# Block lists for a top-1 expert layer: one-hot products in PSUM in place of a table in DRAM

## What is computed

```
x = x + linear_attention(layernorm(x))                 # 0: K^T V form, head of 64
x = x + routed_ffn(layernorm(x)) + shared_ffn(...)     # 0: 8 experts, top 2, inner 352; shared inner 704
x = x + windowed_attention(layernorm(x))               # 1: 16 heads of 16, |i-j| <= 128
logits = xf @ Wg + bg                                  # 1: the last layer
one_hot = one_hot(argmax(logits))
h = gelu(einsum('td,edh->eth', xf, W1)); y = einsum('eth,ehd->etd', h, W2)
out = x + einsum('etd,te->td', y, one_hot)             # 8 experts, top 1, inner 1024
```

## Time and profile before

| | us |
|---|---|
| median of three runs | 1680.56 |
| lowest and highest | 1666.24, 1683.63 |
| the profiled execution | 1689.96 |
| its span on the core | 1688.1 |

### The profile page before, as it was taken

One profiled execution on the slowest core, in us unless ns is written; L12 is line 12 of the kernel. 1 busy time (PEld: TensorE's weight loads), 2 busy tenths in 40 slices (PEclk: granted clock), 3 DMA queues, 4 the chain that ended last, 5 costly groups with the idle time before them and its releaser, 6 DMA issues.

```text
span 1688.1 us, 23687 instructions
## 1 busy us (share of the span) xinstructions
PE 1485.8 (88%) x7821; PEld 1074.7 (64%) x7821; DVE 694.9 (41%) x2367; ACT 458.3 (27%) x769; POOL 481.8 (29%) x568
## 2 busy tenths in 40 slices
PE   7999999999999998988887888888968897688896
PEld 4666655677777764555655555555646786588886
DVE  5643355233333333567775666656543011000000
ACT  1111110112211111145544443535334411111111
POOL 2100000342222215134343343524233432333331
PEclk9998999999999999989998988879878998799999
DMA  9201000111222112335434344434233866678784
GB/s 336 83 17 50 9 0 1 40 61 61 62 63 63 59 53 76 92 106 147 119 114 92 111 98 131 105 110 115 73 79 121 243 174 211 224 291 296 291 312 171
DMA packets 90326, 205.05 MB, mean 121 GB/s; under 512 B 12712, under 2 KB 46783, under 8 KB 80224
## 3 DMA queue, kind: packets, MB, share of 16 engines
q1 hardware_dynamic: 72656, 168.19, 32.0%
q0 software_dynamic: 13184, 32.17, 6.4%
q10 hardware_dynamic: 4368, 3.17, 0.6%
HBM read 151.50 MB, written 52.38 MB: 121 GB/s over the span
## 4 chain that ended last, share of the span: by engine, by line
PE 75%; DMA 8%; DVE 6%; issue 5%; ACT 3%; POOL 1%; SPq 1%; ACTq 1%; DVEq 0%; POOLq 0%
PE psum L699 10%; PE psum L581 9%; PE psum L870 9%; PE psum L880 8%; PE psum L678 5%; PE psum L592 5%; DMA qT<-max_T 4%; PE psum L770 4%; PE psum L725 4%; PE psum L747 3%; PE psum L797 3%; PE psum L508 2%; PE psum L826 1%; PE psum L660 1%; DVE work L1655 1%
## 5 line engine op out<-in xcount | busy, mean ns | idle before, releaser
L1655 DVE CUSTOM_DVE_ANT_0 work<-psum,mask 128x384 bf16<-128x384 f32 (+1 forms) x512 | 230.1, 487 | 183.3 <-PE psum L725 174.6
L1105 ACT ACTIVATE arena<-psum 128x512 f32<-128x512 f32 (+1 forms) x256 | 179.2, 703 | 249.1 <-PE psum L747 237.6
L725 PE MATMUL psum<-kz,qT 96*128 96x384 f32 (+1 forms) x512 | 184.7, 442 | 15.3 <-DVE small L1655 12.3
L699 PE MATMUL psum<-arena,work 128*128 x568 | 186.6, 472 | 3.0 <-ACT work L1017 2.4
L870 PE MATMUL psum<-arena 128*128 128x128 f32 x1248 | 154.9, 285 | 26.5 <-issue 17.1
L747 PE MATMUL psum<-qT,kz 100*128 100x384 f32 (+1 forms) x512 | 136.6, 349 | 39.6 <-DMA qT<-max_T 27.3
L870 PEld LDWEIGHTS psum<-arena 128*128 128x128 f32 x1248 | 150.0, 200 | 31.5 <-issue 22.0
L1731 POOL DMA_INDIRECT work<-normed,token_of x71 | 67.3, 948 | 352.1 <-PE psum L660 210.6
L725 PEld LDWEIGHTS psum<-kz,qT 96*128 96x128 f32 x512 | 97.6, 214 | 98.8 <-issue 50.8
L581 PE MATMUL psum<-arena 128*128 128x512 f32 x320 | 154.3, 628 | 0.0
L1528 DVE TENSOR_TENSOR arena<-psum,arena 128x256 f32<-128x256 f32 x39 | 16.6, 425 | 315.1 <-PE psum L880 315.1
(11 more groups left out here) (216 smaller groups left out, 2021.5 us busy)
## 6 DMA issues: line engine op xcount, KB each, us to landing
arena<-in_w SPq DMA_DIRECT2D x78, 1024.0 KB, 7.8
strips<-hi SPq DMA_DIRECT2D x64, 256.0 KB
kz<-strips SPq DMA_DIRECT2D x64, 192.0 KB, 4.0
qT<-strips SPq DMA_DIRECT2D x32, 384.0 KB, 5.7
results<-work SPq DMA_DIRECT2D x71, 128.0 KB, 1.7
strips<-lo SPq DMA_DIRECT2D x32, 256.0 KB
normed<-work SPq DMA_DIRECT2D x14, 512.0 KB, 3.4
X<-in_x SPq DMA_DIRECT2D x8, 512.0 KB, 9.7
```

The lines of the kernel that those rows point to most:

```text
L699: m = e.matmul(psum[:, pair[u], 0:INTER], xsT0[:, b % 2, c * P:(c + 1) * P], wu0[:, bass.ds(x, 1), c, u * INTER:(u + 1) * INTER], start=(c ...
L725: m = e.matmul(psum[:, bk, at:at + w], qT[0:ROWS_S, slot, half, i * P:(i + 1) * P], kz[slot][0:ROWS_S, hd, lo_key:hi_key], start=True, sto ...
L1105: e.activation(pT[:, j, 2 * half:2 * half + 2, 0:w], src, ACT.Exp, scale=1.0 / E ** 0.5).then_inc(p_exped, 1)
L1655: e.tensor_tensor_reduce(masked[:, n % 2, 0:w], psum[:, bank_of["scores", u, i, hd], at:at + w], mask[:, P - off:P - off + w], 1.0, MASKED ...
```

## The change

The table in DRAM goes, with its clearing, the 32 indirect writes of `pool_place`, the two gathers of `pool_list` and the turning of `pe_list`. In place of them:

- `dve_slots` splits each slot into a place in its block and a block row (`places`), three more small operations a batch.
- `dve_list` loses the six operations that found the table's row and gains four that find each listed block's row number (`block_row`).
- `dve_list_piece` makes, for four token tiles at a time, a one-hot matrix of the places (`one_r`, 128 x 4 x 128) and one of the blocks, twice more multiplied with the tile's number and the row's number (`one_b`, 128 x 4 x 3 blocks). `pe_list_piece` multiplies them into one PSUM bank, four bf16 matmuls a piece. The first list has 5 pieces, one a step (114 to 118), the second 8, two a step (162 to 165); PE does each one step later. `dve_tokens` (steps 120 and 167) takes five dependent small operations in place of two.
- The bank of the first list is bank 2, one of three that the scores use, so the units whose steps overlap it (28 and 29) have two banks.
- SP issues the first weights of block k+1 ahead of the second weights of block k.
- The early blocks are laid later: their first products at 129, 132, 135, 138, 141, 145, 150, 154, 159, 161, 163, 165 (before: 129, 131, 133, 135, 137, 139, 141, 144, 149, 153, 159, 162) and their second at 133, 136, 139, 143, 147, 152, 156, 160, 162, 164, 166, 168 (before: 132 to 145, then 150, 154, 160, 163, 166). The late blocks start at step 170, before at 168.

```diff
-LATE_AT = LISTED_AT[1] + 7
+ROWS_AT = [128, 129, 132, 135, 138, 141, 145, 150, 154, 159, 161, 163]
+UP_AT = ROWS_AT[1:] + [165]
+DOWN_AT = [133, 136, 139, 143, 147, 152, 156, 160, 162, 164, 166, 168]
+LATE_AT = LISTED_AT[1] + 9
+PIECES_AT = [[LISTED_AT[0] + 1 + n for n in range(EARLY_B * TPB // CH)],
+             [LISTED_AT[1] + 1 + n // 2 for n in range(NT // CH)]]
+FETCH_AT += [max(at - 4, PIECES_AT[1][-1] + 2) for at in ROWS_AT[EARLY:]]
...
         def s_ring(u):
-            return (0, 1, 2) if u else (0, 1)
+            return (0, 1) if u in (0, *LIST_UNITS) else (0, 1, 2)
...
+        def pe_list_piece(e, i, n):
+            w, last = 3 * (EARLY, NBLK1 - EARLY)[i], len(PIECES_AT[i]) - 1
+            if n == 0:
+                fill(e, ("list", i), LIST_BANK[i])
+            m = i * len(PIECES_AT[0]) + n
+            e.wait_ge(ones_made, m + 1)
+            for t in range(CH):
+                p = e.matmul(psum[:, LIST_BANK[i], 0:w], one_r[m % 2][:, t, :],
+                             one_b[m % 2].rearrange("p t k b -> p t (k b)")[:, t, 0:w],
+                             start=(n == 0 and t == 0), stop=(n == last and t == CH - 1))
...
+        def dve_list_piece(e, i, n):
...
+            e.tensor_tensor(one_r[m % 2], repeat(count[:, :]), spread(places[:, 0, ts], P), ALU.is_equal)
+            e.tensor_tensor(one, repeat(block_row[:, 0:w]), spread(places[:, 1, ts], w), ALU.is_equal).then_inc(one_hot_made, 1)
+            e.wait_ge(one_hot_made, m + 1)
+            e.tensor_tensor(tile_no, one, spread(count[:, ts], w), ALU.mult)
+            e.tensor_scalar(row, one, row_no[:, 0:1], None, ALU.mult).then_inc(ones_made, 1)
...
-            e.tensor_scalar(slot_of[:, 2, b * TPB:(b + 1) * TPB], slot1, float(NX * NT * P), None, ALU.add).then_inc(slotted, 1)
+            dve_then(e, e.tensor_scalar(slot_int, slot1, float(NX * NT * P), None, ALU.add))
+            e.tensor_scalar(place_i[:, 0, :], slot_int, P - 1, None, ALU.bitwise_and)
+            dve_then(e, e.tensor_scalar(place_i[:, 1, :], slot_int, P.bit_length() - 1, None, ALU.arith_shift_right))
+            e.tensor_copy(places[:, :, b * TPB:(b + 1) * TPB], place_i).then_inc(placed, 1)
...
-                for b, _ in batch(s, GATE_AT + 4):
-                    pool_place(e, b)
-                for i in range(2):
-                    if s == LISTED_AT[i] + 2:
-                        pool_list(e, i)
...
+            sp_first_weights(e, 0)
             for k in range(NBLK1):
-                sp_weights(e, k)
+                if k + 1 < NBLK1:
+                    sp_first_weights(e, k + 1)
+                sp_second_weights(e, k)
```

More of the change, by code:

```diff
@@ L133, in blocks_at, with piece @@
     return [k for k in range(NBLK1) if at[k] + behind == step]
+def piece(step, behind=0):
+    return [(i, n) for i in range(2) for n, at in enumerate(PIECES_AT[i]) if at + behind == step]
 def later(step, behind=0):
@@ L264, in build @@
         y1 = carve(arena, 29952, 3, E)
[L267 to L279, removed]
+        PAD = 2 * NT * P
+        sc1, eq1, cand1, hot1 = (carve(arena, 15168 + TPB * NX * i, TPB, NX) for i in range(4))
+        places = carve(arena, 15296, 2, NT)
+        (so_far, in_batch, n_tokens, n_blocks, up_to, offset, taken, least, jump) = (
+            carve(arena, 15360 + NX * i, NX) for i in range(9))
+        best, pick, rank, slot1 = (carve(arena, 15432 + TPB * i, TPB) for i in range(4))
+        place_i = carve(arena, 15448, 2, TPB).bitcast(I32)
+        block_row = carve(arena, 15456, NBLK1)
+        found = [carve(arena, 15456 + NBLK1 * (1 + i), NBLK1) for i in range(2)]
+        n_int, slot_int = n_tokens.bitcast(I32), slot1.bitcast(I32)
+        NB1 = max(EARLY, NBLK1 - EARLY)
+        ends = carve(work, 4512, NB1, NX)
+        which = carve(work, 4512 + NB1 * NX, NB1)
+        one_r = [carve(work, 4768 + i * CH * P // 2, CH * P // 2).bitcast(BF16)
+                 .rearrange("p (t r) -> p t r", t=CH) for i in range(2)]
+        one_b = [carve(work, 5280 + i * CH * 3 * NB1 // 2, CH * 3 * NB1 // 2).bitcast(BF16)
+                 .rearrange("p (t k b) -> p t k b", t=CH, k=3) for i in range(2)]
         xn = carve(work, 0, 2, TPB, E)
@@ L1513, in dve_tokens @@
         def dve_tokens(e, i):
             n, first = (EARLY, NBLK1 - EARLY)[i], (0, EARLY)[i]
-            bk = bank_of["list", i]
+            tile_no, row, one = (psum[:, LIST_BANK[i], k * n:(k + 1) * n] for k in range(3))
+            f = [found[k][:, 0:n] for k in range(2)]
             e.wait_ge(*done["list", i])
-            e.tensor_copy(token_out[:, first:first + n], psum[:, bk, 0:n])
-            e.tensor_scalar(token_of[:, 1, first:first + n], psum[:, bk, 0:n], NT * P - 1.0, None, ALU.min
-                            ).then_inc(tokens_listed, 1)
+            e.tensor_copy(f[0], row).then_inc(tokens_found, 1)
@@ L1522, in dve_result @@
+            e.wait_ge(tokens_found, 4 * i + 4)
+            e.tensor_copy(token_out[:, first:first + n], f[0]).then_inc(tokens_listed, 1)
         def dve_result(e, k):
@@ L1587, in dve_attention @@
                         dve_list(e, i)
+                for i, n in piece(s):
+                    dve_list_piece(e, i, n)
                 for u, i in unit(s, 0, 4):
```

108 lines of the change are left out of this document (48 added, 60 removed).

## The result

| | before | after |
|---|---|---|
| median, us (four runs each) | 1675.39 | 1589.49 |
| lowest to highest | 1666.24 to 1683.63 | 1582.57 to 1593.92 |
| profiled execution, us | 1689.96 | 1582.57 |

The ratio is 0.9485, 95% interval 0.9416 to 0.9553: 86 us faster, where 54 were forecast, to 1627 us, and 1604 was the lower end of the range. The direction was right and the size was not.

The account below looks back on a forecast made before the run. PE, busy for 88% of the span, was taken as the bound, with its idle time and slow clock to be won. The terms 8 + 9 - 1 + 5 + 14 + 19 = 54 us took 1680.56 to 1627 us, range 1604 to 1658.

Parts of the forecast that it names:

- The writes into the table: In the attention's batches: without 4-byte table writes DMAs land sooner and PE waits less; 9 us won, from 2 to 14.
- Late blocks: Late blocks: first weights issued 3.5 us sooner remove most of PE's 23.1 us of waits before first products; 19 us won.
- First list: At the first list: 15.4 us on offer less 7.5 for pieces, banks and PE's matmuls; net 8, between 3 and 14.
- Early blocks: Stretch from 1290 us: PE's idle of 17 us becomes about 12; change -5 us, between -9 and +5.
- Second list: End of the ranks to first late product: overhead falls from 22 to 8 us; 14 won, between 10 and 17.
- The DMA ceiling (2): Rival, chance 0.2: late blocks limited by bytes, 7.7 to 8.1 us each; only 4 of the 19 us won, 1642 us.
- 4: Rival, chance 0.09: the second list is not covered after all and costs 12 us more; 1639 us.
- 5: Rival, chance 0.03: slower than before, as PE idles more among steps 128 to 160 and gets the lower clock.
- 3: Rival, chance 0.13: DVE bounds the first list, pieces showing in full, and table writes were no culprit, 2 for 9; 1640 us.

Follow-up runs that it names:

- e11: The kernel after with the 32 indirect 4-byte writes put back, at the slots the kernel before used, into a tensor nothing reads: ratio 0.9765.
- e12: The kernel after with 32 indirect writes at the slots the kernel before used, each number written as a 64-byte row: ratio 0.9620.
- e3: The kernel after with five small operations on POOL, about 5 us a batch, and no added DMA: ratio 0.9520.
- e7: The kernel after with two score banks for every unit: ratio 0.9469.
- e8: The kernel after with each piece of the first list making `one_r` three times, 6.8 us more of DVE in all: ratio 0.9530.
- e9: The kernel before with only SP's new weights order, first weights of block k+1 ahead of second weights of block k: ratio 0.9809.
- e6: The kernel after with the early blocks laid as before, the late ones still from step 170: ratio 0.9590.
- e2: The kernel after with four indirect gathers a batch, each reading 128 numbers of 4 bytes from the input: ratio 0.9607.
- e1: The kernel after with four indirect writes a batch, 128 x 4 bytes at first-layer slots, into a table nobody reads: ratio 0.9640.

## Why the prediction was right, and where it failed

- **The writes into the table: the step that failed.** I took 9 us, from 2 to 14, less 1 for DVE. The stretch gave 19 to 36. The reading of SP's queue was right, and e11 against e12 shows it. What I priced was only five waits of PE for DMAs, 14.3 us in all; the maxima's waits in these batches were 16 to 19 us, and 12 to 15 of them went. Two terms I had put at nothing, without a reason: the 5 us by which four writes push POOL's own work back, so that DVE's masks came late (8.6 us of waits, now 2.0), and the clock, by which the same matmuls took 3 to 18 us longer. e3 shows the first in its trace (7.4 us of waits for masks, 4 to 7 us more idle) and not in its medians; the second is a difference of busy times at 0.86 to 0.89 and 0.90 to 0.92 of the clock. The upper end of 14 was no bound, since it was a sum of waits at one clock.
- **Late blocks: mechanism right, size off.** 19 forecast, 24 to 28 measured. I kept back 4 us for late landings, where 1.0 us of idle was left, and left out the clock: idle fell by 21 to 22 us and PE's busy time by 2 to 7. The period of 7.25 came out to the digit, and the weights' landing stayed, 7.9 against 8.1. The order also gains 6 to 7 us in the early blocks, which I had not looked for.
- **First list: right by two errors.** 8 forecast, 7 to 10 measured. By e7 the banks cost nothing, not 2; by e8 the pieces cost their full DVE time at the margin, 6.5 and not 3.5. The two cancel in part, which is luck.
- **Early blocks: right by luck.** 21.7 and 22.5 us less, of which 14.1 moved behind the ranks, so 8 against 5. But 6 to 7 of the 8 are the weights' order (e9), so the layout itself gave 1 to 3, and the gather's wait, forecast at 2 to 3, stayed at 5.32.
- **Second list: right.** 1.4 and 4.7 less with 14.1 more work in it, 16 to 19 against 14. The first late product came 34.7 us behind the end of the ranks (1342.63 to 1377.29); I had 34.5. By e6 nearly all of it is the cover that the layout moves there.
- **What the sum did not have:** 5.4 us at the end.
- **Rivals.** The DMA ceiling (2) fell at 0.98 busy; 4 and 5 did not happen. Of 3, the half on DVE is true at the margin and did not cost the gain; the half on the table writes is refuted by e11 and e12.

In the sum: 54, and beyond it 11 to 28 from the batches, 5 to 9 from the late blocks, 5 from the end, 5 to 8 from the early blocks and the second list. This is 80 to 104, beside 86 in the medians and 103 to 107 between the traces, of which 3 to 9 lie ahead of the first ranks. The edits need not be additive: putting back the real writes (44), the old order (37) and the old layout (15) one by one gives 96.

Open: why before idles 3 to 6 us more in the four batches than e11 (its waits for the maxima are 16 to 19 us, in e11 8.7, and those for masks 8.6 and 2.4, while e11 has 8.2 for ACT); whether isolated 4-byte writes would hold others up; the step at the end. e2's four batches are longer than e1's by PE's busy time alone, 263.8 against 257.1 at the same idle time of 36.8, which is within what traces of one kernel differ by.

## What to carry to other kernels

Price an operation on a shared in-order queue by what it pushes back, not only by the waits that bear its name, and add the clock: here 14 to 21 us less of idle in the batches came with 3 to 18 us less of matmul time, and 21 to 22 in the late blocks with 2 to 7. Small scattered writes that sit side by side should be made rows of 64 bytes, which held nothing up here, or kept out of DRAM. When a load lands in the same time however it is ordered (8.1 and 7.9 us here), look for the place in the queue where it can be issued one product earlier.

## What the runs showed of the hardware

- Indirect DMAs of 128 writes of 4 bytes, most of them to adjacent words, stretched the way from another queue's write to the read behind it from 6.0 us to between 9.8 and 12.7 (e11), at about half that density to between 7.7 and 8.9 (e1); with rows of 64 bytes it stayed at 5.9 to 6.0 (e12).
- A DVE operation of 128x4 took 0.17 us in the median, and 2.18 beside POOL's two-input addition of 128x1024.
- The DMA engines ran at 0.98 busy and 345 GB/s with 1 MB loads while PE was busy 100% at full clock.
- The end of a program with 276 or more indirect DMAs took 5.3 to 7.5 us longer than with 268 or fewer, in 9 traces against 11; the cause is open.
